# A fused transformer block on one core: the values of the last three batches divided by way of tokens, and a norm moved behind a bank copy

## What is computed

```python
# x: (16, 512, 128)
x = x + attn_a(layernorm(x), w_qkv, w_out, b_out)   # 16 heads of 64; softmax of q over channels, of k over tokens
x = x + ffn(layernorm(x), W_r, W_k, W_v, mu_r, mu_k)
x = x + attn_b(layernorm(x), W_Q, W_K, W_V, W_O)    # 16 heads of 8, rope, softmax(q k / sqrt(8)) v
x = x + ffn(layernorm(x), W_r, W_k, W_v, mu_r, mu_k)
# ffn: xr, xk = mixes of x with the token before; sigmoid(xr W_r) * (relu(xk W_k)**2 W_v)
```

## Time and profile before

| | before |
|---|---|
| median of 3 runs | 1057.42 us (1057.36 to 1058.03) |
| the profiled execution | 1057.29 us, span 1055.5 us |
| PE busy | 955.3 us (91%) |
| ACT busy | 765.6 us (73%) |
| DVE busy | 671.1 us (64%) |
| POOL busy | 422.4 us (40%) |
| mean granted TensorE clock | 0.972 of 2.4 GHz |

### The profile page before, as it was taken

One profiled execution on the slowest core, in us unless ns is written; L12 is line 12 of the kernel. 1 busy time (PEld: TensorE's weight loads), 2 busy tenths in 40 slices (PEclk: granted clock), 3 DMA queues, 4 the chain that ended last, 5 costly groups with the idle time before them and its releaser, 6 DMA issues.

```text
span 1055.5 us, 21055 instructions
## 1 busy us (share of the span) xinstructions
PE 955.3 (91%) x8119; PEld 516.9 (49%) x8119; DVE 671.1 (64%) x1488; ACT 765.6 (73%) x879; POOL 422.4 (40%) x306
## 2 busy tenths in 40 slices
PE   5987889999999999999999999999999999798863
PEld 3775535455554545455454545455454545233222
DVE  5666537577675847577675857667675746856433
ACT  4555666878787787878787787878787787485850
POOL 3757252625343352625343352624443351403000
PEclk9999999999999999999999999999999999898985
DMA  5102222223131322223131322223131222232310
GB/s 169 29 12 91 61 69 83 80 75 107 52 114 47 91 74 79 90 71 110 54 112 48 83 78 82 91 71 111 48 103 51 71 81 81 70 91 75 95 41 15
DMA packets 67057, 80.62 MB, mean 76 GB/s; under 512 B 13313, under 2 KB 39810, under 8 KB 66946
## 3 DMA queue, kind: packets, MB, share of 16 engines
q1 hardware_dynamic: 66946, 79.15, 25.5%
HBM read 16.19 MB, written 20.97 MB: 35 GB/s over the span
## 4 chain that ended last, share of the span: by engine, by line
PE 68%; ACT 14%; DVE 9%; issue 3%; POOL 2%; SPq 1%; DMA 1%; ACTq 0%; DVEq 0%
PE PS L1457 18%; PE PS L1274 8%; PE PS L1413 7%; ACT work L599 6%; PE PS L1276 5%; PE PS L1275 5%; PE PS L1330 4%; PE PS L1381 3%; PE PS L1269 3%; PE PS L1374 3%; PE PS L1351 3%; PE PS L1368 2%; ACT hn L626 2%; PE PS L1430 2%; PE PS L1473 2%
## 5 line engine op out<-in xcount | busy, mean ns | idle before, releaser
L599 ACT ACTIVATE work<-PS 128x2048 f32<-128x2048 f32 x208 | 390.6, 1878 | 2.4 <-issue 0.6
L1457 PE MATMUL PS<-work,v 128*32 128x512 f32 x2048 | 278.2, 616 | 6.3 <-DVE U L974 5.2
L593 ACT ACTIVATE work<-PS 128x512 f32<-128x512 f32 x256 | 152.0, 597 | 163.2 <-PE PS L1276 161.0
L398 POOL TENSOR_TENSOR rs<-ve,half_neg 128x4 f32<-128x4 f32 x64 | 65.3, 1021 | 384.7 <-DVE ve L818 384.7
L411 POOL TENSOR_TENSOR work<-work,q_rcp 128x1024 f32<-128x1024 f32 x64 | 121.9, 1905 | 122.7 <-DVE q_rcp L870 122.7
L1274 PE MATMUL PS<-wqk,h1h 128*128 128x512 f32 x256 | 122.7, 479 | 25.7 <-ACT gate L640 13.4
L1413 PE MATMUL PS<-q_st,k_st 32*128 32x512 f32 x832 | 105.6, 496 | 1.8 <-ACT work L599 0.3
L1276 PE MATMUL PS<-wqk,h1l 128*128 128x512 f32 x256 | 102.3, 400 | 0.0
L1275 PE MATMUL PS<-wqk,h1h 128*128 128x512 f32 x256 | 102.2, 399 | 0.0
L867 DVE TENSOR_REDUCE q_sum<-work 128x16 f32<-128x1024 f32 x64 | 77.7, 1214 | 12.0 <-ACT work L593 11.8
L1330 PEld LDWEIGHTS PS<-work 128*64 128x64 f32 x2048 | 65.2, 138 | 41.0 <-ACT work L593 33.9
(11 more groups left out here) (144 smaller groups left out, 1589.3 us busy)
## 6 DMA issues: line engine op xcount, KB each, us to landing
qkv_scratch<-qkv_sb SPq DMA_DIRECT2D x16, 768.0 KB, 3.6
k_st<-k_hi SPq DMA_DIRECT2D x128, 64.0 KB, 2.1
k_st<-k_lo SPq DMA_DIRECT2D x128, 64.0 KB, 2.1
q_st<-q_hi SPq DMA_DIRECT2D x128, 64.0 KB, 2.1
q_st<-q_lo SPq DMA_DIRECT2D x128, 64.0 KB, 2.1
parted<-U SPq DMA_DIRECT2D x64, 128.0 KB, 2.8
xa<-in_attn_a_x SPq DMA_DIRECT2D x16, 256.0 KB, 2.9
xr<-in_attn_a_x SPq DMA_DIRECT2D x16, 256.0 KB, 3.1
```

The costliest lines, as they stand in the source:

```text
L398: pool.tensor_tensor(rs[:, :], ve[:, :], half_neg[:, :], ALU.pow).then_inc(rstd[n].sem, 1)
L593: act.activation((EQ, EK)[r // 2][c % 2][:, (r % 2) * 512:(r % 2) * 512 + 512], PS[:, bank, :], ACT.Exp)\
L599: act.activation(probs[n % 2], PS[:, 0:4, :], ACT.Exp).then_inc(z["s_exp"].sem, 1)
L1457: mm = pe.matmul(PS[32 * h:32 * h + 32, 6, :], v_flat[p][:, kc, at:at + 32], probs[n % 2][:, h, :], start=(n % 8 == 0), stop=(n % 8 == 7), ...
```

## The change

For batches from `LATE = 13` on, the division of the main path goes by way of tokens. Their `part_values` are not issued, and `divide` isn't called. In place of these, `u_transposes` of half 0 at n=15 of the batch's own step and `normalise` of half 0 at the end of DVE's step; in the next step `u_transposes` of half 1 at n=1, `normalise` of half 1 behind `split_h3`, `c_transposes` at n=2 and `cT_copy` on ACT after the exponentials of n=2. Batch 12, which is divided in step 16, keeps the old way. Apart from that, in all steps from 16 on DVE's `pv_copy` of half 0 stands ahead of `ln_norm(3, e, x3, hn2)` and no longer behind it. Holds are added where banks 7 and 4 change hands. The diff (`normalise`, `c_transposes` and `cT_copy` only get an index for their own signals beside the batch):

```diff
--- before.py
+++ after.py
@@ -220,6 +220,8 @@
         FUSED = NB + 4
         SPLIT_FROM = NB - 3

+        LATE = NB - 3
+


         Places = namedtuple("Places", "c1 T M Y h1T h3T pb hT1 k1 r1 kT qT v1 mid")
@@ -331,7 +333,7 @@
                 if there(b):
                     stack_k(z, b, 1)
                     stack_q(z, b, 1)
-                if there(e):
+                if there(e) and e < LATE:
                     part_values(z, e, 1)
                 if there(b):
                     stack_k(z, b, 2)
@@ -348,7 +350,8 @@
                 if there(b):
                     stack_k(z, b, 3)
                     stack_q(z, b, 3)
-                    part_values(z, b, 0)
+                    if b < LATE:
+                        part_values(z, b, 0)
                 if there(l):
                     stack_k(z, l, 0)
                     stack_q(z, l, 0)
@@ -644,8 +647,9 @@
                 hold(act, h1_T, j)
                 act.activation(h1T[p][:, :], PS[:, 4, :], ACT.Copy).then_inc(h1_sb.sem, 1)

-            def cT_copy(z, j):
-                hold(act, z["ct_ps"], j)
+            def cT_copy(z, j, k):
+                hold(act, z["ct_ps"], k)
+                hold(act, z["o_mm"], j - 1)
                 act.activation(cT[:, :], PS[:, 4, :], ACT.Copy).then_inc(z["ct_sb"].sem, 1)

             def t_copy(j, banks=(5, 7)):
@@ -729,6 +733,8 @@
                         exp_scores(z, b, n)
                     if B and not A:
                         exp_scores_split(z, b, n)
+                    if n == 2 and E and e >= LATE:
+                        cT_copy(z, e, e - LATE)
                     if n == 2 and S:
                         t_copy(s)
                     if n == 3 and S:
@@ -777,7 +783,7 @@
             def guarded_b(i):
                 for n in range(16):
                     exp_scores(att[1], i, n)
-                cT_copy(att[1], i)
+                cT_copy(att[1], i, i)
                 scale_mu(ffn[2], i)
                 relu(ffn[2], i)
                 gates(ffn[2], i)
@@ -967,18 +973,20 @@

             def pv_copy(z, b, u):
                 hold(dve, z["pv"], b, 8 * u + 8)
-                if z is att[0]:
+                if z is att[1]:
+                    hold(dve, z["u_T"], b, u - 1)
+                elif b <= LATE:
                     hold(dve, z["c_in"], b - 1)
                 else:
-                    hold(dve, z["u_T"], b, u - 1)
+                    hold(dve, z["u_T"], b - 1 - LATE)
                 dve.tensor_copy(U[u][:, :], PS[:, 6, :]).then_inc(z["pv_sb"].sem, 1)

-            def normalise(z, b, u):
+            def normalise(z, k, u):

                 src = PS[:, 7, :].rearrange("p (c h r) -> p c h r", c=NC, h=8)
-                hold(dve, z["u_T"], b, u + 1)
+                hold(dve, z["u_T"], k, u + 1)
                 dve.reciprocal(den_rcp[:, :, :], src[:, :, :, 1]).then_inc(z["u_norm"].sem, 1)
-                hold(dve, z["u_norm"], b, 2 * u + 1)
+                hold(dve, z["u_norm"], k, 2 * u + 1)
                 dve.tensor_tensor(c_tok[:, :, 64 * u:64 * u + 64].rearrange("p c (h d) -> p c h d", h=8),
                                   src[:, :, :, 0:2 * DB:2], den_rcp[:, :, :].unsqueeze(3).to_broadcast([P, NC, 8, DB]),
                                   ALU.mult).then_inc(z["u_norm"].sem, 1)
@@ -1094,6 +1102,8 @@
                     c_norm(s)
                 if L:
                     split_h3(l)
+                if E and e >= LATE:
+                    normalise(z, e - LATE, 1)
                 if L and draining(i):
                     hold(dve, qkv_st, l - 1)
                     hold(dve, z["roped"], l - 1)
@@ -1104,7 +1114,7 @@
                 if A:
                     hold(dve, ph_exp, a, 2)
                     q_sums(a, 0)
-                if E:
+                if E and e < LATE:
                     divide(z, e)
                 if there(a + 1):
                     ln1_stats(a + 1)
@@ -1122,6 +1132,8 @@
                     p_copy(l, 3)
                 if S:
                     ln_norm(1, s, x1, hn1)
+                if B and draining(i):
+                    pv_copy(z, b, 0)
                 if E and draining(i):
                     ln_norm(3, e, x3, hn2)
                 elif E:
@@ -1129,7 +1141,7 @@
                 if A and not E:
                     hold(dve, ph_exp, a, 10)
                     q_sums(a, 2)
-                if B:
+                if B and not draining(i):
                     pv_copy(z, b, 0)
                 if S and draining(i):
                     scale_and_mix(f1, s)
@@ -1165,6 +1177,8 @@
                     gate_v(f2, e)
                     hold(dve, z["out_st"], e - 1)
                     add_gated(f2, e, x3, out_sb)
+                if B and b >= LATE:
+                    normalise(z, b - LATE, 0)
                 if at_batch(i, NB + 1):
                     norm_columns()

@@ -1463,8 +1477,8 @@
                 hold(pe, z["pv_sb"], b, u + 1)
                 four_transposes(lambda c: U[u][:, c * P:(c + 1) * P], 7).then_inc(z["u_T"].sem, 1)

-            def c_transposes(z, j):
-                hold(pe, z["u_norm"], j)
+            def c_transposes(z, k):
+                hold(pe, z["u_norm"], k)
                 four_transposes(lambda c: c_tok[:, c, :], 4).then_inc(z["ct_ps"].sem, 1)

             def heads_out(z, j):
@@ -1587,7 +1601,19 @@
                     if n == 0 and L and at.h3T == 0:
                         hold(pe, f1["x"], s - 1, 1)
                         hold(pe, f2["x"], e - 1, 1)
+                        if E and e >= LATE:
+                            hold(pe, z["u_norm"], e - LATE, 2)
                         h3_transposes(l)
+                    if n == 1 and E and e >= LATE:
+                        if L:
+                            hold(pe, h3_sp, l)
+                        else:
+                            hold(pe, f2["x"], e - 1, 1)
+                            hold(pe, z["u_norm"], e - LATE, 2)
+                        u_transposes(z, e, 1)
+                    if n == 2 and E and e >= LATE:
+                        hold(pe, f2["gate"], e - 1)
+                        c_transposes(z, e - LATE)
                     if n == 2 and S:
                         if E:
                             hold(pe, h3_sp, l)
@@ -1609,6 +1635,8 @@
                     if at.pb <= n < at.pb + 4 and L:
                         if n == at.pb and S:
                             hold(pe, t_ev, s)
+                        elif n == at.pb:
+                            hold(pe, z["u_norm"], e - LATE)
                         proj_b(l, n - at.pb)
                     if n == 4 and S:
                         attn_out(s, 1 - p)
@@ -1652,7 +1680,7 @@
                         elif L:
                             hold(pe, p_ev, l)
                         else:
-                            hold(pe, f2["x"], e - 1, 1)
+                            hold(pe, z["u_norm"], e - LATE)
                         ffn_T(f2, 3, e)
                     if n == at.r1 and S:
                         if A and B:
@@ -1692,6 +1720,10 @@
                     if n == 15 and A:
                         hold(pe, ph_exp, a, 12)
                         context(a, 2)
+                    if n == 15 and B and b >= LATE:
+                        if E:
+                            hold(pe, f2["x"], e, 1)
+                        u_transposes(z, b, 0)

             def guarded_a(j, p):
                 f = ffn[0]
```

## The result

| | before | after |
|---|---|---|
| median | 1057.36 us (7 runs, 1055.93 to 1058.03) | 1049.40 us (7 runs, 1047.84 to 1053.97) |
| ratio | | 0.9936, 95% interval 0.9923 to 0.9949 |
| profiled execution | 1057.29 us, span 1055.5 | 1047.84 us, span 1046.0 |
| mean granted clock | 0.972 | 0.978 |

Eight microseconds less; 7.3 had been forecast (1050.0). The traced execution of the changed kernel is the shortest of its seven; to see which part of a difference is the change's, the end of the kernel is cut at marks that every trace has: the DVE add that makes x1 of batch 15 (in step 16), and the starts of the four last writes of out_sb. What lies ahead of the first mark is untouched, and in the fourteen traces of this study it took 898.3 to 903.8 us.

A forecast was written before the change was run, and what follows sets the result against it. From step 16 on, a score loop of PE and ACT was taken to bound the kernel, with waits for DVE falling into it. Terms +1.1 − 4.4 − 0.3 − 3.7 = −7.3 us took 1057.3 to 1050.0 us, range 1047.3 to 1053.6.

The forecast's parts named there:

- Step 16: Batch 13's first half: the norm moved behind the copy delays the first FFN's mix, uncovered; +1.1 us.
- 1.3 had been named: Sign in step 16: PE waits some 1.3 us for mixed_k.
- a sign of being wrong: The prediction is wrong if step 16 grows by more than 1.5 us.
- rival (c): Step 16's new gap drops the clock for the rest of the step: 14 us, 1064 us; chance 0.04.
- Step 17: PE's waits before heads_out and the values of n=8 go, ffn_T starts 4.9 us earlier; −4.4 us.
- Step 18: The 0.74 us wait before heads_out goes, cT_copy costs ACT 0.6, ACT sets the step; net −0.3 us.
- rival (a): Transpositions in or beside the score loop don't hide, six sets at 0.5 us: 1053.0 us; chance 0.2.
- Step 19: From bank copy to heads_out, 3.8 us by tokens replaces 7.5 us with the DMA; −3.7 us.
- the chain behind the copy: Step 19: transpositions, normalise, c_transposes and cT_copy between bank copy and heads_out, summed to 3.8 us.
- rival (b): Clock stays at 2.4 GHz in step 19, c_transposes 0.5 and heads_out 0.9 shorter: 1048.6 us; chance 0.15.

The follow-up runs named there:

- e1: The kernel before with only the new order (bank copy ahead of the second FFN's norm), division still by DMA: 1056.20 us, ratio 0.9986.
- e4: The changed kernel with LATE = 15, only batch 15 divided by tokens, and the hold before ffn_T of step 18 as before the change: 1052.07 us, ratio 0.9944.
- e10: The changed kernel plus five matmuls without use in step 16, four before the first FFN's ffn_T and one before its ffn_k: 1046.72 us.
- e11: e3 plus five matmuls without use in step 16, four before the first FFN's ffn_T and one before its ffn_k: 1047.68 us.
- e0: The changed kernel run again without edit, giving the second trace: 1049.63 us, ratio 0.9917 against the kernel before.
- e6: e3 plus 14 matmuls without use in the gaps of step 19: 1046.22 us.
- e3: The changed kernel with the old order (norm ahead of bank copy) in step 16 only: 1047.57 us, ratio 0.9905.
- e2: The changed kernel with the old order of norm and bank copy, division by tokens kept: 1049.28 us.
- e5: e3 with ACT applying the second FFN's norm of step 17 and DVE making only the shift: 1044.85 us, ratio 0.9885.
- e7: e3 with POOL's rope in step 17 waiting for the second FFN's norm and DVE's rope sum following the mix: 1047.55 us.
- e8: e5 with ACT also applying the first FFN's norm of batch 15 in step 16: 1043.28 us, ratio 0.9872.
- e9: e8 plus 11 matmuls without use in step 19: 1043.25 us.

## Why the prediction was right, step by step

**Step 16, +1.1 forecast.** The two traces read +0.87 and +3.55, e1 +0.85 and e4 +1.02. The mechanism is right and its size of 1.1 is confirmed by e10 against e11 and by e4 against the kernel before (PE waited 0.76, 2.15 and 1.18 us for mixed_k in the two traces and e4; 1.3 had been named). But the second trace passes the 1.5 us that the prediction had set as a sign of being wrong. Two things were missed. The new gap before ffn_k ends in the lower clock, for 2.5 us in e0: rival (c), but only until 925 and not to the end of the step. And the meeting of the norm with POOL's rope, which I took as fixed, is a matter of some hundredths of a microsecond and is worth 2.3 us at the bank copy and 1.1 at the end of the step (e6 against e3). In the first trace it came out well and paid for the clock, so the +0.87 that looks like the forecast is luck. The transpositions at n=15 hid, normalise moved h3_transposes by about 0.3 (0.23 us of PE waiting for the h norm).

**Step 17, −4.4 forecast.** −4.9 and −4.8 in the two traces. The parts came as told: heads_out at full clock with no wait, the copy first, a gap of 2.37 us (2.6 forecast) before ffn_T. ffn_T came 4.6 us earlier (4.9 forecast), and what stands behind it was 0.3 and 0.2 us shorter, where the forecast had it half a microsecond longer for the clock: two misses that partly cancel. PE did not come back from the gap at 1.2 GHz as told: ffn_T took 0.63 us, and the clock fell only behind it, until about 965. How long it stays down is what the forecast could not know: behind the same gap the same instructions took 15.11 us in e3 and 17.63 in e10.

**Step 18, −0.3 forecast.** +0.04. The 0.74 us of waiting before heads_out went, and cT_copy on ACT and the transpositions took the same back; ACT sets this step. ACT put the 0.60 us of cT_copy between the exponentials as priced, and a second set of transpositions, that of n=1, showed on the chain. The changed kernel's PE:

```profile
981.44 0.66 PE L1283 MATMUL PS<-ident,U 128*128 128x128 f32 x4
982.03 0.51 PE L1444 MATMUL PS<-q_st,k_st 32*128 32x512 f32 x4
```

and ACT, which waited 0.66 us for these scores:

```profile
982.63 1.02 ACT L607 ACTIVATE work<-PS 128x1024 f32<-128x1024 f32 x1 [0.66 <-PE PS L1444]
```

So rival (a) held for one set of six, at 0.5 us.

**Step 19, −3.7 forecast.** −4.7 and −4.6 in the traces, −5.2 and more where heads_out ran at full clock. The term that was mis-sized is the chain behind the copy: 3.18 us instead of 3.8, of which 0.47 is c_transposes, priced at 1.2 GHz by the row after the gap of step 17. It took 0.63; the clock held to about 1019.5, as the windows of the changed kernel show (columns as in the earlier trace rows):

```profile
1016.00:1018.00 2.00, 0.94 (x8) 0.42 (x4) 0.81 (x2) 0.00 (x0) 0.00 (x0) 1.00 0.11 31
1018.00:1020.00 2.00, 0.63 (x4) 0.42 (x4) 0.67 (x2) 0.49 (x1) 0.00 (x0) 0.88 0.00 0
1020.00:1022.00 2.00, 1.75 (x8) 1.78 (x8) 0.00 (x0) 0.11 (x1) 0.00 (x0) 0.50 0.00 0
```

In e2, e3, e4, e5, e7 and e10 it held over heads_out too (1.13 to 1.23 us), which is rival (b); what decides between the two is not shown. Another 0.4 us stand behind heads_out, which the prediction had called unchanged: ffn_v took 1.55 us in the first trace and 1.91 before, with full clock back earlier within it.

**The sum.** +0.9 − 4.9 + 0.0 − 4.7 = −8.7 us between the marks in the first trace, +3.6 − 4.8 + 0.0 − 4.6 = −5.8 in the second; the medians differ by 8.0 in the first comparison and by 8.0 in the second (1057.6 to 1049.63). The forecast of −7.3 is inside, with step 18 and 19 missed by 0.3 and 0.9 in opposite directions. The mechanisms held in the main in all four steps; that the median also lies within 0.7 us of the forecast rests in part on such errors cancelling, and on a spread of step 16 of which it knew nothing.

## What to carry to other kernels

Before an instruction is moved ahead of another in a hand-written order, the engine's wait at each place is the price: the same swap of copy and norm cost 1.1 us in step 16, where the norm had stood in idle time, and gained 2.1 up to ffn_T in step 17, where it had stood in the way. Do such a move step by step, not for all steps of a kind. When DVE's small operations between SBUF tiles take as long as POOL's big ones beside them, giving them to an engine with ports of its own helps (2.7 us from e3 to e5); making POOL wait instead (e7) only moved the wait.

## What the runs showed of the hardware that I had not expected

The same instructions, behind the same 2.37 us gap of TensorE, went on at 2.4 GHz in one kernel's trace and at 1.2 GHz in another's, at a cost of 2.5 us. The Trainium skill, "TensorE: Matmul & The Clock Gate", section "What's actually happening", says that the point of transition varies from run to run, and the traces agree: step 16 of e8 and e9 is a second such pair (31.69 and 33.23 us). How much of the spread of the times comes from it is not shown: the changed kernel's seven runs lie 6 us apart (1047.84 to 1053.97), but the seven of the kernel before, with gaps as long, only 2.1. A DVE add with two SBUF inputs was stretched by POOL from 1.21 to 2.04 us, and a shift of 128x4 beside the rope took 2.25 (e5), out of its way 0.15 (e8).
